# A graph network layer on one core: both gathers and both blocks of the next group's transposes placed behind the seventh sub-convolution

## The reference

```python
h = jnp.maximum(_layernorm(x), 0.0)
# inside the layer, x is h and xc its transpose
c = relu(bn1(conv1d(xc, conv1_w, 0)))
c = bn2(conv1d(c, conv2_w, 8))                 # 17 taps along the nodes
x_conv = transpose(relu(c + xc))
s = x @ w_se.T + b_se                          # 3 features for each node
A = exp(-(squared distance of s_n and s_m)) * adj
x_nmp = A @ relu(x @ w_msg.T + b_msg)
gi = concat([x_conv, x_nmp]) @ w_ih.T + b_ih
gh = x @ w_hh.T + b_hh
r, z = sigmoid(gi_r + gh_r), sigmoid(gi_z + gh_z)
n = tanh(gi_n + r * gh_n)
out = x_input + (1 - z) * n + z * x
```

## Time and profile before

| what | value |
|---|---|
| median of 3 runs | 306.49 us (305.3 to 307.34) |
| profiled execution | 305.3 us, span 303.4 us |
| TensorE matmul busy | 280.9 us, 93% of the span |
| VectorE busy | 229.9 us, 76% |
| ScalarE busy | 177.5 us, 59% |
| GpSimd busy | 89.1 us, 29% |
| mean granted TensorE clock | 0.994 |

### The profile page before, as it was taken

The page is one execution under the profiler, slowest core; times in us unless marked ns, Lnnn a source line. Parts: engine busy times, 40 slices in busy tenths (PEclk is TensorE's granted clock), DMA queues, the critical chain, the costliest instruction groups (busy, mean ns, idle before and its releaser), DMA issues.

```text
span 303.4 us, 5275 instructions
## 1 busy us (share of the span) xinstructions
PE 280.9 (93%) x1880; PEld 254.4 (84%) x1880; DVE 229.9 (76%) x471; ACT 177.5 (59%) x336; POOL 89.1 (29%) x158
## 2 busy tenths in 40 slices
PE   0486999999999999999999999999999999999990
PEld 0266998899888998899988998899988998899880
DVE  4489976796797886796797886796797876776455
ACT  2868566657557566657556566657556566652341
POOL 4817330362205530362205530362205530220000
PEclk9999999999999999999999999999999999999997
DMA  7500030017000530017000430017000510021001
GB/s 255 230 35 0 14 130 2 0 26 252 1 3 0 151 128 1 2 29 249 2 0 2 145 134 0 4 24 252 2 0 2 145 65 0 0 87 54 2 7 62
DMA packets 6509, 18.96 MB, mean 62 GB/s; under 512 B 850, under 2 KB 980, under 8 KB 6356
## 3 DMA queue, kind: packets, MB, share of 16 engines
q1 hardware_dynamic: 6336, 18.62, 18.9%
q10 hardware_dynamic: 148, 0.01, 0.0%
HBM read 14.43 MB, written 4.19 MB: 61 GB/s over the span
## 4 chain that ended last, share of the span: by engine, by line
PE 86%; DVE 5%; ACT 4%; POOL 2%; DMA 1%; issue 1%; SPq 0%; DVEq 0%; POOLq 0%
PE ps L793 24%; PE ps L795 23%; PE ps L794 23%; PE ps L826 5%; PE ps L858 4%; PE ps L802 2%; ACT hn L374 2%; DVE wt_lo L573 2%; PE ps L823 2%; POOL rstd L267 1%; DMA xin<-x_nm 1%; PE ps L837 1%; PE ps L848 1%; DVE stats L552 1%; DVE v_lo L623 0%
## 5 line engine op out<-in xcount | busy, mean ns | idle before, releaser
L793 PE MATMUL ps<-v_hi,wt_hi 128*128 128x256 f32 x320 | 93.6, 292 | 1.6 <-issue 1.4
L795 PE MATMUL ps<-v_hi,wt_lo 128*128 128x256 f32 x320 | 90.7, 283 | 0.0
L794 PE MATMUL ps<-v_lo,wt_hi 128*128 128x256 f32 x320 | 90.3, 282 | 0.0
L793 PEld LDWEIGHTS ps<-v_hi,wt_hi 128*128 128x128 f32 x320 | 60.9, 190 | 3.0 <-issue 2.1
L794 PEld LDWEIGHTS ps<-v_lo,wt_hi 128*128 128x128 f32 x320 | 61.1, 191 | 0.3
L795 PEld LDWEIGHTS ps<-v_hi,wt_lo 128*128 128x128 f32 x320 | 60.7, 190 | 0.0
L374 ACT ACTIVATE hn<-xin,nmr,rstd 128x128 f32<-128x128 f32 x64 | 25.5, 480 | 20.8 <-POOL nmr L269 20.8
L333 POOL COPY hg<-hf 128x512 f32<-128x512 f32 x16 | 19.5, 1219 | 51.0 <-ACT hf L385 51.0
L308 POOL CAST slots<-s_sb 128x48 fp32r<-128x48 f32 x8 | 1.9, 241 | 96.6 <-ACT s_sb L434 96.6
L793 PE MATMUL ps<-h_hi,wt_hi 128*128 128x512 f32 x64 | 26.2, 410 | 0.7 <-DVE h_lo L580 0.7
L795 PE MATMUL ps<-h_hi,wt_lo 128*128 128x512 f32 x64 | 25.8, 403 | 0.0
(11 more groups left out here) (118 smaller groups left out, 638.5 us busy)
## 6 DMA issues: line engine op xcount, KB each, us to landing
mask<-adj_t SPq DMA_DIRECT2D x8, 512.0 KB, 3.3
xt<-x_t SPq DMA_DIRECT2D x8, 512.0 KB, 4.0
out<-gate SPq DMA_DIRECT2D x16, 256.0 KB, 4.1
xin<-x_nm SPq DMA_DIRECT2D x7, 512.0 KB, 3.7
w<-w_conv SPq DMA_DIRECT2D x1, 1088.0 KB, 6.6
gate<-w_gate SPq DMA_DIRECT2D x1, 576.0 KB, 7.5
xin<-x_nm SPq DMA_DIRECT2D x2, 256.0 KB, 2.9
w_a<-w_in SPq DMA_DIRECT2D x1, 130.0 KB, 3.8
```

The lines of the kernel that those rows point to most:

```text
L793: pe.matmul(dst, wt_hi[:, blk, :], hi, start=start, stop=False)
L794: pe.matmul(dst, wt_hi[:, blk, :], lo, start=False, stop=False)
L795: return pe.matmul(dst, wt_lo[:, blk, :], hi, start=False, stop=stop)
```

## The change

Sub-convolution 6 is written ahead of the first gather, so that the gather, transposes, gather, transposes stand in one block between sub-convolutions 6 and 7. ACT's and DVE's lists follow: `m_shared(g, 2)` now stands directly behind `m_shared(g, 1)`, and `add_shared(g, 1)` ahead of `n_low(g, 0, 5)`.

```diff
@@ -520,10 +520,10 @@
                 if ahead:
                     ln_rows(g + 1)
                 m_shared(g, 1)
+                m_shared(g, 2)
                 n_high(g, 0, 5)
                 if ahead:
                     h_rows(g + 1, 0, 6)
-                m_shared(g, 2)
                 n_high(g, 1, 7)
@@ -763,10 +763,10 @@
                 add_shared(g, 0)
                 join_y(g, 0, 0)
                 join_y(g, 0, 1)
+                add_shared(g, 1)
                 n_low(g, 0, 5)
                 if ahead:
                     h_low(g + 1, 0)
-                add_shared(g, 1)
                 n_low(g, 1, 7)
                 join_y(g, 1, 0)
@@ -939,10 +939,10 @@
                 sub_conv(g, 5)
+                sub_conv(g, 6)
                 gather(g, 0, 5)
                 if ahead:
                     h_transpose(g + 1, 0, 6)
-                sub_conv(g, 6)
                 gather(g, 1, 7)
                 if ahead:
                     h_transpose(g + 1, 1, 3)
```

## The result

The changed kernel takes 312.84 us (median of 6 runs, 312.17 to 313.4) where the kernel before takes 306.35 (305.16 to 307.34): slower by 6.5 us, ratio 1.0195, 95% interval 1.016 to 1.023. The forecast was 311.5 us, 5.5 us more. Its profiled execution took 312.17 us, span 310.3.

A forecast was written before the change was run, and what follows sets the result against it. TensorE, busy for 93% of the span, was taken to bound the kernel. The terms 1.25 + 4.62 - 0.4 gave 5.5 us more, 310.8 or 312.0 us by base; forecast 311.5 us, range 310.5 to 313.2, widened to 309.3 and 314.

The forecast's parts named there:

- The wait and its place: TensorE at sub-convolution 6 waits for ACT's `mbs1` seven times, 0.6 to 0.8 us each, about 1.5 in group 0.
- Groups 1 to 6: Sub-convolution 6 could start at 107.49 instead of 106.72 in group 2: 0.77 us in each group, 4.62 us in all.
- Fewer changes of kind: One passage from transposes to a sub-convolution less per group on TensorE: 0.05 us saved in each of eight, 0.4 in all.
- Group 0: Sub-convolution 6 cannot start before 39.62; gather and transposes now run after that wait: 1.25 us more.
- ACT behind the stall, DVE, POOL: Later `n_high`, `h_rows`, `h_low` and `hg` copies behind sub-convolution 6 stay in time, `gates_h` covered by 1.1 us: no cost.
- Rival 1: POOL's layer norm part gets shorter, so no stall in the middle groups: +0.6 us, 307.1 us; chance 6%.
- Rival 2: ACT's or DVE's second burst becomes late, `gates_h` waits for `hf`: at 0.5 us beyond cover 3.5 more, 315; chance 4%.
- Rival 3: TensorE's clock falls after the new stalls: 1.3 us in each of seven groups, +9, 320 us; chance 3%.
- The base: Starting time for the added 5.5 us: profiled execution 305.3 gives 310.8, median 306.49 gives 312.0; 311.5 taken between.

The follow-up runs named there:

- experiment 2: Changed kernel with the copy `mbs1` between the seventh and eighth `hn` instruction instead of behind all eight: 309.57 us, ratio 1.0102.
- experiment 6: Changed kernel with the order gather, gather, transposes, transposes behind sub-convolution 6: 312.29 us, ratio 1.0178.
- experiment 1: Changed kernel with ACT's copy `mbs1` ahead of the eight `hn` instructions instead of behind them: 306.44 us, ratio 0.9999.
- experiment 4: Changed kernel with TensorE's order as in the kernel before, so only ACT's and DVE's lists changed: 305.4 us, ratio 0.9983.
- experiment 10: Kernel before with `mbs1` ahead of `hn`, and in group 0 sub-convolution 1 moved ahead of the factor transposes, 2 ahead of the distances: 304.29 us, ratio 0.9917.
- experiment 9: Kernel of experiment 1 with, in group 0, sub-convolution 1 moved ahead of the factor transposes and 2 ahead of the distances: 304.05 us, ratio 0.9914.
- experiment 5: Changed kernel with sub-convolution 6 moved between the first gather and its transposes: 306.41 us, ratio 1.001.
- experiment 8: Kernel before with ACT's copy `mbs1` ahead of the `hn` instructions, TensorE's order untouched: 306.25 us, ratio 0.9994.

## Why the prediction was right, and where it was off

*The wait and its place.* Right. It is `mbs1`, late behind `hn`, seven times, and experiment 2 ties the time to that copy. About 1.5 us was forecast for the wait of group 0. It is 0.61 in the changed kernel's own profile, since TensorE came there late in that execution, and 1.55 in experiment 6, which starts like the kernel before.

*Groups 1 to 6.* The lateness was forecast at 0.77 and is 0.76 to 0.78. It came again in each group, as it should if the layer norm chain moves with TensorE. But the groups are 0.85 us longer, not 0.77.

*Fewer changes of kind.* This is the term that was mis-sized: forecast -0.05 us in each of eight groups, measured +0.07 in seven. There was nothing to save: the 0.08 us of the transposes' last part only moved, from the start of sub-convolution 6 into the block (experiment 6), and without a wait the new order takes the 4.00 us of the old one (experiment 1). And a start after a wait is followed by 0.19 us where 0.12 was usual, although a sub-convolution stood ahead of it (110.14 to 110.33). The row for that was at hand in group 0; I took it as a reason to halve a saving where it was a cost. In group 7, with no wait, it makes no difference whether the gathers stand together or around sub-convolution 6: 3.13 us from the end of sub-convolution 5 to the start of sub-convolution 7 in both kernels. The measured 0.5 us more and the forecast 0.4 us less make 0.9 us, which is what the forecast lacked: 5.5 and 6.4.

*Group 0.* Forecast 1.25. With the start of the kernel before, from the start of sub-convolution 6 to that of sub-convolution 7 it took 2.74 us before and takes 4.06 in experiment 6: 1.32. The 0.07 over 1.25 is the last part of the transposes, which had lain under the wait. Sum: 1.32 + 6 x 0.85 = 6.4 us, the difference of the two spans with equal starts. In the changed kernel's own profile the clock fell at the start, and TensorE came to the wait later. Sub-convolution 6 starts 0.46 us later than in the kernel before, 40.08 and 39.62, so the spans differ by 6.9. The price of group 0 thus hangs on the start, which the prediction did not have: where TensorE comes late, the kernel before does not wait there either, and group 0 costs the 0.85 us of the others. The span of the changed kernel is 5.8 us above that of experiment 4, whose start is of this kind (310.3 and 304.5). The 6.5 us between the medians compares runs whose starts differ.

*ACT behind the stall, DVE, POOL.* Right to cost them at nothing: 1.4 us of cover at `gates_h` where 1.1 was forecast. The last `join_y` ends at 118.17 and ACT turns to `xc_hi` at 118.62, 0.45 us apart where the forecast had 0.05 (115.9 and 115.95). Experiment 4 shows no cost either.

*Rival 1* did not come: POOL's part kept its length, and `hn` starts behind 2.42 us of waiting as before. *Rival 2* did not come. *Rival 3* did not come at the new stalls: 0.62 us of idle time, and the next distances are 0.12. A fall of the clock exists in this program, though, behind the idle time of 3 us at its start.
The Trainium skill ("TensorE: Matmul & The Clock Gate", "A second HAM failure mode: psum-queue depth-cycling") has short pauses between groups of matmuls, when they come often enough, make the clock go back and forth; at seven pauses of 0.6 us, 35 us apart, no row here shows it.

*The base.* The prediction said that the runs of before spread by 2 us for no reason that the profile shows, and took 311.5 us as a value between two bases. One profile could not show it; the profiles together do, in part at least: it is the start of the program.

## What to carry to other kernels

When work is moved out from between two instructions of the busiest engine, ask what the second one waits for and by how much that is early. Here it was 0.62 us early under a cover of 1.25, and 5.5 of the 6.4 us of loss could be read off before the run. A late release cost its lateness (0.77) plus the restart (0.07), in every round of the loop. The mend can lie in another engine's list. Here the short copy that frees a buffer went ahead of the long block that nobody needed yet, and the loss was gone; on the kernel before, where the cover still stood, the same edit gained nothing that could be measured.

## What the hardware showed that I had not expected

- TensorE's clock can fall behind one single wait: from 0.12 to 0.21 us for each matmul of 256 columns behind an idle time of 3.0 us, with 0.66 granted in that stretch; behind 1.71 us and behind 0.6 us it did not. Behind 2.35 us it fell in experiment 10 and not in experiment 9, so the length of the idle time alone does not settle it.
- An engine that is faster at first can end later: where sub-convolution 0 ran at full clock from a start near 23.6 us, TensorE reached its wait sooner, lost the clock there, and came to the first gather of group 0 at 39.27 to 39.43 us in experiments 4, 5 and 8, in place of 37.91.
- At 23.60 to 26.50 us in the kernel before, the granted clock read 1.00 while the matmuls ran at the 1.2 GHz level. For the level, distances of starts are the safer row.
